# Encoder values projected token-major and carried to three head bands by SBUF-to-SBUF transfers

## Chip, core and metric

The kernel runs on one core of a Trainium2 chip. The metric is the device time of one execution in microseconds (us), lower is better. Before the change the median of three runs is 821.42 us (821.26 to 821.55).

## What is computed

Sixteen images of 37 tokens (one class token and 36 patches), 256 features, go through a patch embedding, a causal attention block with rotary positions, a mixture of 16 experts, a six-layer encoder and a block whose weights are rounded to four bits. The change lies almost wholly in the encoder. Its attention, cut to what matters:

```python
for l in range(LAYERS):                      # 6
    keys = concatenate([past, x], axis=1)    # past is one row of zeros
    q = (x @ Wq.T + bq).reshape(B, T, 16, 16)
    k = (keys @ Wk.T + bk).reshape(B, T + 1, 16, 16)
    v = (keys @ Wv.T + bv).reshape(B, T + 1, 16, 16)
    attn = softmax(where(valid, q k / 4, neg))
    o = (attn v).reshape(B, T, C) @ Wo[l].T + bo[l]
    x = _ln(x + o, ln1_g[l], ln1_b[l])
    ff = gelu(x @ W1[l].T + b1[l]) @ W2[l].T + b2[l]
    x = _ln(x + ff, ln2_g[l], ln2_b[l])
```

## The kernel before

Everything is kept feature-major: 256 features are two chunks of 128 partitions, the tokens lie in the free dimension. The batch is cut into two halves of 8 images (296 tokens, `NHALF`). The encoder is a chain of phases. `phase(x, y)` does the attention of one half (`x`) together with the first normalisation, the hidden layer and the second normalisation of the other half (`y`), so that each half's dependent steps lie beside the other's matrix products. After an entry phase with attention alone (`phase((0, 0), None)`, from 317.21 us), eleven phases have both parts: six with x = half 1, y = half 0 (from 344.25 to 697.54 us) and five with x = half 0, y = half 1 (from 379.67 to 662.44 us). The first kind is called heavy below, since GpSimd also splits W1 and W2 in it, the second light. A last phase has no attention.

Each engine has its own program, in the order in which it is written, and semaphores tie them. fp32 products are made of three fp32r products (high by high, low by high, high by low), so one 128x296 output takes six matmuls. Up to the first feed-forward product a phase with both parts goes:

- TensorE: values `w` (12 matmuls, `project_v`, L807), q of chunk 0 (6), mean of the normalisation (`ln_mean_of`, L725), k0, q1, k1 (18), variance (`ln_var_of`, L735), 16 transposes of the values (`turn_v`, L812), broadcast of the reciprocal (`ln_bcast_of`, L750), two pairs of scores (`scores`, L825), then `up_first` (L1308). The rest is hidden layer, two more pairs of scores, `down`, transposes of the probabilities, values by probabilities (`values`, L861) and the output projection (L877).
- VectorE: the residual sum R and RSUM of y (L2805, L2706), small copies (L2601 to L2609), centring (`ln_centre`, L2094), evacuation of q0 and q1 with three masks each (L2736), reciprocal (L2100), two masked evacuations of the transposed values (`spread_values`, L2111), gain (`scale_gain`, L2712) and low part of the stream (L2582), two more `spread_values`, then maxima, shifts and sums of the softmax.
- ScalarE: `values_out` (L1547) writes each value three times, with a hole for the zero key, into VT; then square (L1531), keys 0, root (L1536), keys 1, high part of the stream (L1842), gelus, exponentials.
- GpSimd: half of the split of W1, the sum of the squares (L2016), the rest of the split, four low parts of the hidden layer (L2054), `normalise` (L1975).
- SyncE: nothing but weight loads in these phases (L694 to L702).

The three copies of a value (`JH` = 3) are rows g*38 to g*38+36 of Ve, each multiplied by a mask that leaves the heads of its band. PSUM banks of the phases are a ring of six, handed out in the order of `phase_order` (L112); `free_bank` (L759) waits for the reader of the job that had the bank before.

Of the kernel before, what the change touches and what calls it, by code (L numbers as in the profile page):

```python
# [16 lines left out]
F32 = mybir.dt.float32  # L17
# [20 lines left out]
KROWS = JH * KEYS  # L38
SCOLS = C * KROWS
# [70 lines left out]
def phase_order(x, y):  # L110
# [12 lines left out]
    att("w", 0, 1)  # L123
# [3 lines left out]
    att("v", 0, 1, 2, 3)  # L127
# [27 lines left out]
def build(nc, a):  # L155
# [8 lines left out]
    with ExitStack() as ctx:  # L164
# [41 lines left out]
        rmask = sb("rmask", [P, JH])  # L206
# [40 lines left out]
        v_, at = cut(at, C * HB * KROWS)  # L247
        VT = v_.rearrange("p (c b g k) -> p c b g k", c=C, b=HB, g=JH)
        ATT_N = at
# [3 lines left out]
        XHL = over("XHL", ARENA_BASE, at, [P, 2, 2, C, NHALF])  # L253
        XH, XL = XHL[:, 0], XHL[:, 1]
        at += 4 * C * NHALF
# [173 lines left out]
        x_ready = sem("x_ready")  # L429
        q_ready, k_ready, v_ready, o_ready = (sem(n) for n in ("q_ready", "k_ready", "v_ready", "o_ready"))  # L430
# [177 lines left out]

        block = ctx.enter_context(nc.Block())
# [3 lines left out]
        def _(sp):  # L613
# [89 lines left out]

            sp.wait_ge(fp4_stored, 32)
# [10 lines left out]
        def _(pe):  # L715
# [91 lines left out]
            def project_v(r, plan, h, pairs, high_count, low_count):  # L807

                two_products(r, plan, [("w", 2 * h + c) for c in range(C)], [pairs(c) for c in range(C)],
                             high_count, low_count)  # L810

            def turn_v(r, plan, h, which=range(4)):  # L812

                for i in which:
                    key = ("v", 4 * h + i)

                    free_bank(r, plan, key, ("w", 2 * h + 1) if i == 0 else None)
                    o = bank_of(plan, key)
                    for b in range(2):
                        for c in range(C):  # L820
                            last = nc.tensor.transpose(o[0:KROWS, b * D + c * P:b * D + (c + 1) * P],
                                                       VT[:, c, 2 * i + b].rearrange("p g k -> p (g k)"), ident)
# [23 lines left out]
            def transpose_probs(r, plan, p, constants=0):  # L846
# [5 lines left out]
                for i in range(2):  # L852
                    for c in range(C):
                        col = (i * C + c) * QROWS
                        last = nc.tensor.transpose(
                            o[0:KROWS, col:col + QROWS],
                            Pr[0:QROWS, (2 * p + i) % PSLOTS, JH * c:JH * (c + 1), :].rearrange("p g k -> p (g k)"),
# [2126 lines left out]
```

## Time and profile before

| | us |
|---|---|
| median of three runs | 821.42 |
| span of the profiled execution | 819.1 |
| PE busy | 801.5 (98%) |
| PE weight load busy | 751.4 (92%) |
| DVE busy | 633.9 (77%) |
| ACT busy | 460.6 (56%) |
| POOL busy | 251.6 (31%) |

The granted clock of TensorE is full over the whole span. A timeline row gives the start, the time from the start of the first to the end of the last instruction, engine, line, output and inputs with their form, and count. Matmuls overlap each other in the pipeline, so what one costs TensorE is the distance of two starts, not its own duration (300 ns for one that follows every 137 ns). A time in brackets is idle time before the row and who ended it. PE is TensorE, DVE VectorE, ACT ScalarE, POOL GpSimd.

### The profile page before, as it was taken

To read this page: it belongs to the slowest core of one execution; us is meant where nothing else is said; L and a number is where in the kernel's file an instruction comes from. 1 tells how busy PE (TensorE), PEld (TensorE's weight loads), DVE (VectorE), ACT (ScalarE), POOL (GpSimd) and SP (SyncE) were. 2 spreads that over 40 slices of the span, in tenths; PEclk is the share of its full clock that TensorE was granted. 3 is DMA by queue.
4 is the path that set the end of the run, shared out by engine and by line. 5 is a ranking of instruction groups with operands and counts; after the bars stand their busy time and mean duration, and the time that the engine had idled before them with its cause. 6 is when DMAs were issued, how large, how long until landed. Compare 5 with 4: busy or idle time off the path is not lost.

```text
span 819.1 us, 16629 instructions
## 1 busy us (share of the span) xinstructions
PE 801.5 (98%) x6060; PEld 751.4 (92%) x6060; DVE 633.9 (77%) x1287; ACT 460.6 (56%) x829; POOL 251.6 (31%) x297
## 2 busy tenths in 40 slices
PE   9999999999999999999999999999999999999988
PEld 8998789999999999899999989999998999999758
DVE  5786693778778876778797887878778787876796
ACT  4386424433333336585786777667687767745421
POOL 0002120410111100364366147335525623633020
PEclk9999999999999999999999999999999999999999
DMA  5010946998889812010210021031012103010001
GB/s 191 1 52 1 373 124 253 328 323 310 317 309 337 321 53 107 1 40 14 100 44 0 17 98 38 13 102 38 4 39 72 38 13 102 26 82 1 1 0 30
DMA packets 18290, 88.36 MB, mean 108 GB/s; under 512 B 3120, under 2 KB 7472, under 8 KB 12240
## 3 DMA queue, kind: packets, MB, share of 16 engines
q1 hardware_dynamic: 18256, 87.90, 30.4%
q8 instruction: 22, 0.36, 0.2%
q14 instruction: 12, 0.10, 0.0%
HBM read 85.05 MB, written 2.84 MB: 107 GB/s over the span
## 4 chain that ended last, share of the span: by engine, by line
PE 47%; issue 23%; POOL 18%; DVE 8%; ACT 3%; DMA 1%; POOLq 0%; SPq 0%; DVEq 0%; ACTq 0%
PE bank L1139 14%; POOL W_L L2000 7%; PE bank L1176 6%; POOL HF_L L2058 4%; POOL arena L1981 3%; POOL WQKV_L L2000 3%; PE bank L746 2%; PE bank L872 2%; PE bank L1185 2%; PE bank L722 2%; PE bank L1049 2%; PE bank L788 1%; POOL SQ L2019 1%; PE bank L1123 1%; PE bank L1490 1%
## 5 line engine op out<-in xcount | busy, mean ns | idle before, releaser
L1139 PE MATMUL bank<-arena 128*128 (+1 forms) x1024 | 117.8, 274 | 0.0
L1139 PEld LDWEIGHTS bank<-arena 128*128 128x128 f32 x1024 | 117.4, 192 | 0.0
L1981 POOL TENSOR_TENSOR arena<-arena,srec 111x456 f32<-111x456 f32 x56 | 52.3, 962 | 125.1 <-DVE srec L2153 125.1
L2000 POOL TENSOR_TENSOR W_L<-LW,W_H 128x256 fp32r<-128x256 f32 x96 | 68.5, 752 | 36.9 <-DVE XHL L2589 33.5
L2058 POOL TENSOR_TENSOR HF_L<-arena,HF_H 128x296 fp32r<-128x296 f32 x48 | 43.8, 937 | 76.7 <-ACT HF_H L1896 76.7
L788 PE MATMUL bank<-XHL,W_H 128*128 128x296 f32 x288 | 65.1, 307 | 0.0
L1896 ACT ACTIVATE arena<-bank,vec 128x296 f32<-128x296 f32 x96 | 48.8, 509 | 20.4 <-PE bank L788 15.4
L2012 POOL TENSOR_TENSOR QW<-QW,arena x14 | 22.4, 1600 | 119.0 <-DVE QW L2490 65.6
L1330 PE MATMUL bank<-HF_L,W_H 128*128 128x296 f32 x192 | 57.4, 299 | 0.0
L1330 PE MATMUL bank<-HF_H,W_H 128*128 128x296 f32 x192 | 57.4, 299 | 0.0
L1330 PE MATMUL bank<-HF_H,W_L 128*128 128x296 f32 x192 | 57.3, 299 | 0.0
L872 PE MATMUL bank<-arena 114*128 114x111 f32 x448 | 55.1, 276 | 0.8 <-issue 0.7
L872 PEld LDWEIGHTS bank<-arena 114*128 114x128 f32 x448 | 53.1, 192 | 2.6 <-issue 1.3
L2165 DVE TENSOR_SCALAR OB<-bank,lvec 96x148 f32<-96x148 f32 x144 | 51.1, 368 | 5.7 <-PE bank L872 3.3
L841 PEld LDWEIGHTS bank<-arena 128*111 128x111 f32 x448 | 52.4, 175 | 1.1
L841 PE MATMUL bank<-arena 128*111 128x114 f32 x448 | 52.7, 260 | 0.0
L2149 DVE TENSOR_REDUCE ssum<-arena 111x12 f32<-111x456 f32 x56 | 32.1, 608 | 23.8 <-ACT arena L1545 23.6
L788 PEld LDWEIGHTS bank<-XHL,W_H 128*128 128x128 f32 x288 | 48.3, 188 | 0.3
L1896 ACT ACTIVATE HF_H<-bank,vec 128x296 fp32r<-128x296 f32 x96 | 48.3, 503 | 0.0
L788 PE MATMUL bank<-XHL,WQKV_H 128*128 128x296 f32 x192 | 45.4, 311 | 0.0
L2138 DVE TENSOR_REDUCE smax<-bank 111x12 f32<-111x456 f32 x56 | 33.9, 622 | 14.4 <-PE bank L841 14.3
L2497 DVE TENSOR_TENSOR EWD_L<-arena,EWD_H 128x2048 fp32r<-128x2048 f32 x16 | 36.9, 2304 | 10.0 <-ACT EWD_H L1758 10.0
(276 smaller groups left out, 2205.4 us busy)
## 6 DMA issues: line engine op xcount, KB each, us to landing
arena<-ew_in SPq DMA_DIRECT2D x16, 2048.0 KB, 9.0
arena<-ew_in SPq DMA_DIRECT2D x16, 1024.0 KB, 7.0
LW<-lw_in SPq DMA_DIRECT2D x12, 1024.0 KB, 5.0
arena<-route SPq DMA_DIRECT2D x32, 185.0 KB, 3.2
LW<-lw_in SPq DMA_DIRECT2D x6, 768.0 KB, 4.3
fp_weights<-arena SPq DMA_DIRECT2D x1, 2048.0 KB, 6.4
arena<-fp_weights SPq DMA_DIRECT2D x1, 2048.0 KB, 7.2
arena<-patches_in SPq DMA_DIRECT2D x2, 864.0 KB, 7.4
```

Source lines behind the costliest of these rows:

```text
L788: last = mm(o, w, x, start=(i == 0), stop=(i == len(pairs) - 1))
L841: last = mm(o[0:QROWS, col:col + KROWS], Qe[:, h, c, bb].rearrange("p s q -> p (s q)"), Ke[:, at_half(plan, h), c, bb].rearrange("p g k -> ...
L872: last = mm(o[:, i * QROWS:(i + 1) * QROWS], Ve[0:KROWS, at_half(plan, h) * HB + b % HB, c * P:(c + 1) * P], PTr[0:KROWS, b % PSLOTS, c, : ...
L1139: last = mm(o[:, m * CAP:(m + 1) * CAP], w[:, kc, mi * P:(mi + 1) * P], xg(kc, e), start=(kc == 0), stop=(kc == C - 1))
L1176: last = mm(bank[4][0:CAP, 0:D], hid_part, w_part, start=(m == 0 and i == 0), stop=(m == EM - 1 and i == 2))
L1330: last = mm(bank_of(plan, keys[c])[:, 0:NHALF], w, moving, start=(m == 0 and i == 0), stop=(m == FM - 1 and i == 2))
L1896: last = f(out[:, m, :], bank_of(plan, ("f1", FM * hy + m))[:, 0:NHALF], ACT.Gelu, bias=vec[:, 3 * C + m:3 * C + m + 1])
L1981: nc.gpsimd.tensor_tensor(v, v, srec[0:QROWS, s:s + 2, :].unsqueeze(3).to_broadcast([QROWS, 2, C * JH, KEYS]), ALU.mult).then_inc(p_ready, 1)
L2000: last = nc.gpsimd.tensor_tensor(low[:, cols], value[:, cols], high[:, cols], ALU.subtract)
L2058: nc.gpsimd.tensor_tensor(HF_L[:, m, :], HF[:, m, :], HF_H[:, m, :], ALU.subtract).then_inc(hl_ready_pool, 1)
L2165: return v.tensor_scalar(dst, src, bias(c)[lo:hi, :], None, ALU.add)
L2497: v.tensor_tensor(EWD_L[s][:, :, :], value, EWD_H[s][:, :, :], ALU.subtract).then_inc(wd_low, 1)
```

## The change

In the encoder the values are projected with the tokens as the stationary operand. Three tiles of three images (the last of two) give 114, 114 and 77 rows (the last three of each are the pad of a 40-row block), each tile 6 matmuls that move 256 weight columns. ScalarE copies them to VTOK. SyncE then issues nine transfers per phase, from SBUF to SBUF: for each of the three bands g and each image i of a tile, 40 rows (37 tokens and 3 that the mask zeroes) to rows g*40 of Ve. The bands are 40 rows apart instead of 38 (`KPAD`), so probabilities and their transposes have 120 rows, with zeroed pads. The images of the first four are masked in place by GpSimd, the last four by VectorE, in one operation each. `turn_v`, `spread_values` and `values_out` remain for the first attention block only. The order in a phase changes too: TensorE makes q0 and k0 together, then q1, mean, k1, two tiles of values, variance, the last tile, scores of pair 0, broadcast, scores of pair 1. VectorE evacuates q0 ahead of the centring. ScalarE puts the square between keys 0 and keys 1 and the root behind keys 1. The jobs `v` leave the encoder's bank ring. SyncE loads the next layer's q, k, v weights when the last value tile is done.

```diff
@@ -36,6 +36,10 @@
 JH = 3
 QROWS = JH * T
 KROWS = JH * KEYS
+KPAD = 40
+VROWS = JH * KPAD
+VTILES = -(-HB // JH)
+XPAD = NHALF + KPAD - T + 1
...
@@ -120,11 +124,10 @@
         if y is not None:
             jobs.extend((kind, y * PER_ROUND[kind] // 2 + i) for i in items)
 
-    att("w", 0, 1)
     for c in range(C):
         att("q", c)
         att("k", c)
-    att("v", 0, 1, 2, 3)
+    att("w", 0, 1)
     att("s", 0, 1)
     for i in range(4):
...
-        v_, at = cut(at, PSLOTS * SCOLS)
-        Pr = v_.rearrange("p (s g k) -> p s g k", s=PSLOTS, k=KEYS)
+        v_, at = cut(at, PSLOTS * C * VROWS)
+        Pr_rows = v_.rearrange("p (s g k) -> p s g k", s=PSLOTS, k=KPAD)
+        Pr = Pr_rows[:, :, :, 0:KEYS]
...
+        VTOK = v_[:, 0:VTILES * D].rearrange("p (t v) -> p t v", t=VTILES)
...
+        V_MOVED = JH * JH * 16
+
+        def first_or_last_values(g4):
+
+            return Ve[0:VROWS, 4 * g4:4 * g4 + 4, :].rearrange("p b (c d) -> p (b c) d", c=C)
+
+        def value_mask():
+
+            return vmask[0:VROWS, :].unsqueeze(1).to_broadcast([VROWS, 4 * C, P])
+
+        def tile_rows(t):
+
+            return (min(JH, HB - t * JH) - 1) * T + KPAD
...
+            def move_values(h, r):
+
+                sp.wait_ge(w_ready, nth("w", 2 * h + 1, r))
+                for g in range(JH):
+                    for i in range(JH):
+                        tiles = -(-(HB - i) // JH)
+                        sp.dma_start(Ve[g * KPAD:(g + 1) * KPAD, i:HB:JH, :], VTOK[i * T:i * T + KPAD, 0:tiles, :]
+                                     ).then_inc(v_landed, 16)
+
+            move_values(0, 1)
             with sp.Fori(1, LAYERS) as l:
-                sp.wait_ge(filled["v"], nth("v", 7, l))
+                move_values(1, l)
+                sp.wait_ge(filled["w"], nth("w", 3, l))
                 load_layer(l)
                 sp.wait_ge(filled["p"], nth("p", 3, l))
                 load_rest(l, "wo", LW_AT["wo"], WO_N, ld_wo)
+                move_values(0, l + 1)
                 sp.wait_ge(filled["f1"], nth_enc("f1", 15, l))
                 load_rest(l, "w1", LW_AT["w1"], W1_N, ld_w1)
                 sp.wait_ge(filled["f2"], nth_enc("f2", 3, l))
                 load_rest(l, "w2", LW_AT["w2"], W2_N, ld_w2)
 
+            move_values(1, LAYERS)
             sp.wait_ge(fp4_stored, 32)
...
+            def values_by_token(r, plan, h, i):
+
+                key = ("w", 2 * h + i)
+                free_bank(r, plan, key)
+                o = bank_of(plan, key)
+                for t in range(2 * i, min(2 * i + 2, VTILES)):
+                    lo, rows, at = t * QROWS, tile_rows(t), t % 2 * D
+                    pairs = [(0, kc, w) for kc in range(C) for w in (WQKV_H, WQKV_L)] + [(1, kc, WQKV_H) for kc in range(C)]
+                    for k, (part, kc, w) in enumerate(pairs):
+                        last = mm(o[0:rows, at:at + D], XHL[:, part, h, kc, lo:lo + rows], w[:, kc, 2 * D:3 * D],
+                                  start=(k == 0), stop=(k == len(pairs) - 1))
+                last.then_inc(filled["w"], 1)
...
-                    if c == 0:
+                    if c == 0 and plan.first:
                         pe.wait_ge(v_ready, nth("v", 4 * h + 3, r))
+                    elif c == 0:
+                        pe.wait_ge((first_masked, last_masked)[g4 % 2], 2 * r + (h - 1))
...
-                    project_v(rx, plan, hx, lambda c: qkv_pairs(2, c), high_count, low_count)
-
-                    def queries_or_keys(c, *kinds):
-                        for kind in kinds:
-                            g = 0 if kind == "q" else 1
-                            key = (kind, 2 * hx + c)
-                            free_bank(rx, plan, key)
-                            products(bank_of(plan, key)[:, 0:NHALF], qkv_pairs(g, c)
-                                     ).then_inc(filled[kind], 1)
-
-                if x:
-                    if y:
-                        pe.wait_ge(proj_added, nth("p", 2 * hy, ry))
-                    queries_or_keys(0, "q")
+                    def query_or_key(kind, c):
+                        key = (kind, 2 * hx + c)
+                        free_bank(rx, plan, key)
+                        products(bank_of(plan, key)[:, 0:NHALF], qkv_pairs("qk".index(kind), c)).then_inc(filled[kind], 1)
+
+                    two_products(rx, plan, [("q", 2 * hx), ("k", 2 * hx)], [qkv_pairs(g, 0) for g in range(2)],
+                                 high_count, low_count)
+                    query_or_key("q", 1)
...
                 if x:
-                    queries_or_keys(0, "k")
-                    queries_or_keys(1, "q", "k")
+                    query_or_key("k", 1)
+                    values_by_token(rx, plan, hx, 0)
...
                     ln_var_of((ly, 0), hy, ones_d)
                 if x:
+                    values_by_token(rx, plan, hx, 1)
                     if entry:
                         ln_bcast_of(LN_ENC, 1)
-                    turn_v(rx, plan, hx)
+                    scores(rx, plan, p0)
...
                 if x:
-                    for i in range(2):
-                        scores(rx, plan, p0 + i)
+                    scores(rx, plan, p0 + 1)
                 if y:
...
-                    values_out(rx, plan, hx)
-                if y:
+                if y and not x:
                     ln_square((ly, 0), hy)
-                if not x:
                     ln_square(LN_FINAL, 0)
...
+                    def values_by_token_out(i):
+
+                        act.wait_ge(filled["w"], nth("w", 2 * hx + i, rx))
+                        o = bank_of(plan, ("w", 2 * hx + i))
+                        tiles = min(2, VTILES - 2 * i)
+                        rows = tile_rows(2 * i)
+                        f(VTOK[0:rows, 2 * i:2 * i + tiles, :].rearrange("p t v -> p (t v)"), o[0:rows, 0:tiles * D], ACT.Copy
+                          ).then_inc(w_ready, 1)
+
                     keys(0)
+                    if y:
+                        ln_square((ly, 0), hy)
+                    keys(1)
                 if y:
                     ln_root((ly, 0), hy)
                 if x:
-                    keys(1)
+                    if y:
+                        act.wait_ge(v_landed, V_MOVED * (lx * 2 + hx))
+                    for i in range(2):
+                        values_by_token_out(i)
                 if y:
                     act.wait_ge(vec_ready, ly + 1)
                     high_stream(hy, xa_count(ly, hy, 0), 0)
...
+            def mask_first_values(h, l):
+
+                pool.wait_ge(v_landed, V_MOVED * (l * 2 + (h + 1)))
+                v = first_or_last_values(0)
+                nc.gpsimd.tensor_tensor(v, v, value_mask(), ALU.mult).then_inc(first_masked, 1)
...
-                    ln_centre((ly, 0), hy)
-                if not x:
-                    ln_centre(LN_FINAL, 0)
+                    if not x:
+                        ln_centre((ly, 0), hy)
+                        ln_centre(LN_FINAL, 0)
                 if x:
                     hx, lx = x
                     rx = lx + 1
                     p0 = HB // 2 * hx
                     for c in range(C):
+                        if y and c == 1:
+                            ln_centre((ly, 0), hy)
...
                     ln_recip((ly, 0), hy)
-                if x:
-                    spread_values(rx, plan, hx, (0, 1))
...
                 if x:
-                    spread_values(rx, plan, hx, (2, 3))
-                if x:
                     row_max(rx, plan, p0)
                     if isinstance(lx, int) and hx + lx == 0:
                         dve.wait_ge(fp4_stored, 32)
+                        link(clear_probability_pads())
...
                     shift(rx, plan, p0 + HB // 2 - 1)
                     if y:
                         low_hidden(2, 3)
+                    dve.wait_ge(v_landed, V_MOVED * (lx * 2 + (hx + 1)))
+                    late = first_or_last_values(1)
+                    v.tensor_tensor(late, late, value_mask(), ALU.mult).then_inc(last_masked, 1)
                     for i in range(0, HB // 2, 2):
```

## Rows read from the trace of the kernel before

**Rows 1.** The page, part 1: busy time, share of the span and instructions.

```profile
PE 801.5 (98%) x6060; PEld 751.4 (92%) x6060; DVE 633.9 (77%) x1287; ACT 460.6 (56%) x829; POOL 251.6 (31%) x297
```

**Rows 2.** Timeline of TensorE in the light phase that starts at 591.76.

```profile
591.76 0.49 PE L803 MATMUL bank<-XHL,WQKV_H 128*128 128x296 f32 x1
...
594.41 0.66 PE L728 MATMUL bank<-RSUM,ones_d 128*128 128x296 f32 x2
...
597.57 0.88 PE L746 MATMUL bank<-ones_d,SQ 128*128 128x64 f32 x6
598.28 1.91 PE L821 MATMUL bank<-const,arena 128*114 128x128 f32 x16
600.03 0.49 PE L755 MATMUL bank<-const,ln_rs 128*128 128x128 f32 x3
...
602.25 0.38 PE L803 MATMUL bank<-XHL,W_H 128*128 128x296 f32 x1
```

**Rows 3.** Timelines of VectorE, ScalarE and GpSimd in the same light phase.

```profile
595.11 0.77 DVE L2097 TENSOR_TENSOR CN<-R,bank 128x592 f32<-128x592 f32 x1 [0.47 <-PE bank L728]
595.80 3.05 DVE L2736 TENSOR_SCALAR arena<-bank,lvec,qmask 128x296 f32<-128x296 f32 x6
...
600.56 0.96 DVE L2716 SCALAR_TENSOR_TENSOR XD<-CN,lvec,bank 128x296 f32<-128x296 f32 x2 [0.35 <-PE bank L755]
...
601.12 0.97 ACT L1849 ACTIVATE XHL<-XD,vec 128x296 fp32r<-128x296 f32 x2 [0.90 <-DVE XD L2716]
...
596.69 0.82 POOL L2019 TENSOR_TENSOR SQ<-SQ 128x296 f32<-128x296 f32 x1 [5.06 <-ACT SQ L1534]
```

**Rows 4.** Timeline of TensorE in the experts: first and last of 24 matmuls over 256 columns.

```profile
301.66 0.28 PE L1176 MATMUL bank<-EWD_L,HH_H 128*74 128x256 f32 x1
...
304.25 0.28 PE L1176 MATMUL bank<-EWD_H,HH_L 128*74 128x256 f32 x1
```

**Rows 5.** Timelines of three engines in the heavy phase that starts at 556.14.

```profile
562.19 0.88 PE L746 MATMUL bank<-ones_d,SQ 128*128 128x64 f32 x6
...
564.66 0.49 PE L755 MATMUL bank<-const,ln_rs 128*128 128x128 f32 x3
...
566.88 0.38 PE L803 MATMUL bank<-XHL,W_H 128*128 128x296 f32 x1
...
559.73 0.77 DVE L2097 TENSOR_TENSOR CN<-R,bank 128x592 f32<-128x592 f32 x1 [0.24 <-PE bank L728]
...
565.86 0.97 ACT L1849 ACTIVATE XHL<-XD,vec 128x296 fp32r<-128x296 f32 x2 [1.01 <-DVE XD L2716]
```

**Rows 6.** Timeline of TensorE: last pair of scores, a heavy and a light phase.

```profile
571.46 0.40 PE L834 MATMUL bank<-amask 128*111 128x456 bf16 x1
...
606.61 0.40 PE L834 MATMUL bank<-amask 128*111 128x456 bf16 x1
```

**Rows 7.** Timelines of VectorE and GpSimd ahead of the softmax sums, light phase.

```profile
608.91 0.83 DVE L2722 TENSOR_TENSOR HF_L<-arena,HF_H 128x296 fp32r<-128x296 f32 x2
...
610.21 1.58 DVE L2722 TENSOR_TENSOR HF_L<-arena,HF_H 128x296 fp32r<-128x296 f32 x2
613.93 1.16 DVE L2149 TENSOR_REDUCE ssum<-arena 111x12 f32<-111x456 f32 x2 [2.14 <-ACT arena L1545]
...
609.64 3.62 POOL L2058 TENSOR_TENSOR HF_L<-arena,HF_H 128x296 fp32r<-128x296 f32 x4 [12.13 <-ACT HF_H L1896]
615.31 3.69 POOL L1981 TENSOR_TENSOR arena<-arena,srec 111x456 f32<-111x456 f32 x4 [2.05 <-DVE srec L2153]
```

**Rows 8.** Timelines of TensorE and GpSimd in the entry phase.

```profile
317.21 0.39 PE L803 MATMUL bank<-XHL,WQKV_H 128*128 128x296 f32 x1
...
331.69 4.14 POOL L1981 TENSOR_TENSOR arena<-arena,srec 111x456 f32<-111x456 f32 x4 [37.17 <-DVE srec L2153]
```

**Rows 9.** The page, part 6: DMA issues, KB of each, us from issue to landing.

```profile
LW<-lw_in SPq DMA_DIRECT2D x6, 768.0 KB, 4.3
...
arena<-patches_in SPq DMA_DIRECT2D x2, 864.0 KB, 7.4
```

More of the change, by code:

```diff
@@ L251, in build @@
         HF = v_.rearrange("p (m t) -> p m t", m=FM)
-        XHL = over("XHL", ARENA_BASE, at, [P, 2, 2, C, NHALF])
-        XH, XL = XHL[:, 0], XHL[:, 1]
-        at += 4 * C * NHALF
+        XHL = over("XHL", ARENA_BASE, at, [P, 2, 2, C, XPAD])
+        XH, XL = (XHL[:, k, :, :, 0:NHALF] for k in range(2))
+        at += 4 * C * XPAD
         W1_H = over("W1_H", ARENA_BASE, at, [P, C, HID])
@@ L805, in two_products, with turn_v @@
                             last.then_inc(filled[key[0]], 1)
[L807 to L812, printed above, removed]
+            def values_by_token(r, plan, h, i):
[9 more added lines that the diff above has]
+                last.then_inc(filled["w"], 1)
+            def turn_v(h, which):
                 for i in which:
                     key = ("v", 4 * h + i)
-                    free_bank(r, plan, key, ("w", 2 * h + 1) if i == 0 else None)
-                    o = bank_of(plan, key)
+                    free_bank(0, BLOCK0, key, ("w", 2 * h + 1) if i == 0 else None)
+                    o = bank_of(BLOCK0, key)
                     for b in range(2):
                         for c in range(C):
-                            last = nc.tensor.transpose(o[0:KROWS, b * D + c * P:b * D + (c + 1) * P],
+                            last = nc.tensor.transpose(o[0:VROWS, b * D + c * P:b * D + (c + 1) * P],
                                                        VT[:, c, 2 * i + b].rearrange("p g k -> p (g k)"), ident)
@@ L2239, in masks @@
                 link(v.tensor_scalar(qmask[:, 1, :], qmask[:, 0, :], HD ** -0.5, None, ALU.mult))
-                three_bands(rmask, KEYS)
+                p1 = cst("iota_col")
+                for g in range(JH):
+                    link(v.tensor_scalar(vrow[:, g:g + 1], p1, float(g * KPAD), None, ALU.is_gt))
+                    last = v.scalar_tensor_tensor(vrow[:, g:g + 1], p1, float(g * KPAD + T), vrow[:, g:g + 1],
+                                                  ALU.is_le, ALU.mult)
+                link(last)
                 for j in range(JH):
                     dst = vmask[:, :].rearrange("p (i d) -> p i d", d=HD)[:, j::JH, :]
-                    last = v.tensor_copy(dst, rmask[:, j:j + 1].unsqueeze(2).to_broadcast([P, dst.shape[1], HD]))
+                    last = v.tensor_copy(dst, vrow[:, j:j + 1].unsqueeze(2).to_broadcast([P, dst.shape[1], HD]))
                 link(last)
@@ L2349, in _ @@
             ln_recip(LN_ATT0, 1)
[L2350 removed]
+            spread_values(0, (0,))
             block0_scale(1)
             rope(0, 1, (1,))
[L2353 removed]
+            spread_values(0, (1,))
             block0_low(1)
[L2355 removed]
+            spread_values(0, (2, 3))
             rope(1, 0, (0,))
@@ L2373, in _ @@
             row_recip(0, 2)
-            spread_values(0, BLOCK0, 1, (0,))
+            spread_values(1, (0,))
             row_sum(0, 3)
             row_recip(0, 3)
-            spread_values(0, BLOCK0, 1, (1, 2))
+            spread_values(1, (1, 2))
             row_max(0, BLOCK0, 4)
@@ L2394, in _ @@
             row_recip(0, 7)
-            spread_values(0, BLOCK0, 1, (3,))
+            spread_values(1, (3,))
             dve.wait_ge(proj_added, 2)
```

62 lines of the change are left out of this document (33 added, 29 removed).

## Prediction

> **What bounds the kernel now.** I read the page's busy line first. TensorE is busy 98% of the span [rows 1], so the first guess is that each matmul column taken away is time won. Then I read the timelines of one phase, engine by engine, for what TensorE waits on at the end of each step. In a light phase it runs from 591.76 to the first feed-forward product at 602.25, 10.49 us, nearly without a gap [rows 2]. Three chains of the normalisation cross this stretch: mean (594.41), variance (597.57), broadcast (600.03). Between mean and variance VectorE centres at 595.11, ScalarE squares, GpSimd adds from 596.69 to 597.51, and the variance starts at 597.57 [rows 2, 3]: 2.46 us from centring to variance, and TensorE starts it 0.06 us after GpSimd is done. So this chain, not the 18 matmuls beside it, sets the start already. Between broadcast and feed-forward VectorE scales at 600.56 and ScalarE makes the high part from 601.12, two operations in 0.97 [rows 3]. Its first half lands at about 601.63, so the feed-forward product could start at about 601.73, 1.70 us after the broadcast started. It starts at 602.25, so two pairs of scores hide this chain with 0.5 us to spare. The question for the change is what hides these chains in the new order.
>
> **Part 1, matmuls.** Removed in each of 12 phases: 12 matmuls over 296 columns for the values, at the distance of 0.137 us that such matmuls keep in this trace; I work it out from the 18 matmuls plus mean between 594.41 and 597.57, less the mean's 0.5 and the wait of 0.2 (2.46/18) [rows 2]. That is 1.64 us. Removed too: 16 transposes, 600.03 - 598.28 = 1.75 us [rows 2]. Added: 18 matmuls over 256 columns. 23 distances of such take 304.25 - 301.66 + 0.118 = 2.71, 0.118 each [rows 4], so 2.12 us. Net -1.27 us, and -1.23 with one more switch from fp32 to fp32r. If nothing else bound, 12 x 1.23 = 14.8 us would be won.
>
> **Part 2, the variance in a light phase.** VectorE is idle for 0.47 before it centres at 595.11, so it is free at 594.64 [rows 3]. The new order puts q0 ahead of the centring: three of the six operations that take 3.05 together, 1.5 us [rows 3]. q0 is filled by then (10 matmuls after 591.76, about 593.3), so it runs 594.64 to 596.15. The centring moves by 1.04, and the variance, 2.46 behind it, to 598.61. TensorE would be ready much sooner: from the mean it has 6 matmuls (0.82) and two value tiles (12 x 0.118 = 1.42) in the place of 18 (2.46), so 0.22 earlier than today's 597.37, at 597.15. It waits 1.5 us. The 1.75 us of transposes were behind the variance and don't help here.
>
> **Part 3, from the variance to the feed-forward.** Behind 598.61 come variance 0.71 (598.28 - 597.57), third value tile 0.78 (6 x 0.118 and the switch), one pair of scores 0.98 (half of 602.25 - 600.03 - 0.33, rounded up with its bf16 mask product), then the broadcast at 601.08. The root and reciprocal fit in (ScalarE has keys 1 from about 597.6 to 599.1, before the variance is done at 599.3). Only one pair of scores is left behind the broadcast, 0.33 + 0.98 = 1.31 us, against the 1.70 us that the chain needs. The feed-forward starts at 601.08 + 1.70 = 602.78, 0.53 later than today [rows 2, 3]. From there the order and the matmuls are as before, and TensorE is full. So a light phase gets longer by 0.5 us: saving 1.23 becomes a loss. Five phases: +2.6.
>
> **Part 4, heavy phases.** Here VectorE is idle only 0.24 before 559.73 [rows 5], so 1.5 us of q0 push the centring by 1.27, the variance from 562.19 to 563.46, the broadcast to 563.46 + 2.47 = 565.93. The high part starts 1.20 after the broadcast (565.86 - 564.66) and its half takes 0.5, so 1.81 to the product: 567.74 against 566.88, +0.86 [rows 5]. One gain: the fourth pair of scores starts 4.58 behind the first feed-forward product in the heavy phase, 4.36 in the light one [rows 5, 6, 2]. The 0.22 is a wait for a shift that VectorE does behind the last `spread_values`. Those are gone and the wait with them. 0.64 x 6 = +3.8.
>
> **Part 5, what is hidden.** ScalarE loses two operations over 888 elements and gains 512 + 256, and it waits for nothing there. VectorE loses four evacuations of 512, and gains one mask over 1024 elements from SBUF to SBUF. Its price: 0.83 for two of 296, 1.58 for the same two while GpSimd works [rows 7], so 1.3 to 2.7 us; I take 1.3, since it is mostly one long operation. It stands behind the low parts that end at 611.79, ahead of the sums that wait until 613.93: 2.14 us of cover [rows 7]. GpSimd's mask is priced by `normalise`, 3.69/4 = 0.92 per 456 elements, 2.1 us for 1024 (by the fp32r subtractions of 3.62/4 per 296, 3.1). It has 12 us of idle ahead of 609.64 in a light phase, and behind it 2.05 before `normalise` [rows 7]. I cost both at nothing; without cover they cost what they take, up to 2 us a phase. The small pads and masks before the encoder: +0.1.
>
> The wait that is new is for the nine transfers. 960 KB of 1 KB runs have no row of their kind. Nearest below: 768 KB in 4.3 us, so 5.4. Nearest above, runs of 1152 B: 864 KB in 7.4, so 8.2 [rows 9]. I take 7, nearer to the short runs, from the first issue. In a light phase the last value tile is copied by about 600.7, so they land at 607.7, before GpSimd's 609.64 and VectorE's 611.79. Queued behind them on SyncE is only the load of the next q, k, v weights, which nobody needs before the phase ends.
>
> The row of 768 KB and that of 864 KB spread over 128 partitions. The Trainium skill (DMA: Bandwidth & Descriptors, "Why a DMA increments its semaphore by 16 and not by 1") says that a transfer uses the largest number of DMA engines up to 16 that divides its outer dimension, so 40 rows get ten. An estimate by that page, 5.4 x 1.6 = 8.6 us, would still be covered in eleven phases. No row of the trace before has 40 rows.
>
> **Part 6, the entry phase.** It has no feed-forward to hide anything. Today `normalise` starts at 331.69 [rows 8]. New: q, k and three tiles are done about 317.21 + 24 x 0.137 + 2.12 = 322.6, copied by 323.3, landed by 330.3. VectorE masks 330.3 to 331.6, then sums (1.16) and reciprocals to about 333.1; GpSimd masks to 332.4, and if the two shut each other out, to 333.7. So `normalise` starts at 333.1 to 335.2 and all that follows is later by that much: +1.4 to +3.5, and with 5.4 or 8.2 us of transfer -0.2 to +4.7. I take +2.4.
>
> The two rows of 0.83 and 1.58 show that VectorE and GpSimd slow each other on SBUF [rows 7]. The Trainium skill (SBUF — State Buffer, "SBUF: two separate sides") calls it an exclusive lock for the whole instruction when a VectorE operation has two SBUF inputs; by that the masks here run one after the other, the upper half of the range just given.
>
> **Sum.** 2.6 + 3.8 + 0.1 + 2.4 = +8.9 us. The profiled span is 819.1, 2.3 below the median of 821.42, and none of that is touched. 821.4 + 8.9 = 830.3.
>
> **Rivals.** (a) *The busy share decides*, faster: the waits of parts 2 and 3 don't arise and 14.8 is won, less 2.4 at the entry: 809. It needs the variance's input 1.5 us earlier than the rows say, at 597.15 in the light phase; even with q0 for nothing it comes at 597.57. Chance 0.07. (b) *q0 doesn't push the centring*, faster: if VectorE has q0 done before the mean is there, the variance stays at 597.57, the feed-forward starts at 597.57 + 2.47 + 1.70 = 601.74, -0.5 a light phase, -0.4 - 0.2 a heavy one, -6.1 + 2.5: 818. It decides at a q0 start of 593.6, when VectorE still adds residuals. Chance 0.13. (c) *Half of the push*, 821 to 825, the chain after the broadcast shorter than read: 0.15. (d) *Values come late in every phase*: if the transfers take over 11 us or the masks 2 us more than covered, each of 11 phases waits 1 to 2 us at the sums: +11 to +22 on the forecast, 841 to 852. For it: short runs, nine issues, one queue; against it: 9 us between copy and first need. Chance 0.15. The forecast, 825 to 836, has 0.5.
>
> **Numbers.** The range runs from 817 to 839: it holds the forecast, (b), (c) and the near end of (d). 0.2% is 1.6 us, about what a measurement of this kernel can tell from no change. Faster: (a), (b): 0.2. Same: part of (c): 0.1. Slower: 0.7.
>
> **What would show it.** In the timeline after: an idle of about 1.5 us before the variance matmuls, q0's evacuation ahead of the centring that waits for nothing, feed-forward starts about 11.0 and 11.6 us into the phase (now 10.5 and 10.7); phases of 35.6 and 36.2 us. Wrong if the centring starts within 0.1 us of the mean's end, or if TensorE waits at the probabilities' transposes for over 0.5 us a phase (d).

## Result and profile after

The changed kernel takes 849.0 us (848.6 to 849.3) against 821.3 us before, a ratio of 1.0336 with a 95% interval of 1.0322 to 1.0351. It is slower, as forecast, but by 27.7 us where 8.9 were worked out, and outside the range. The profiled span is 847.3 us, 28.2 more than before [rows 1]. The page's busy line of the changed kernel:

```profile
PE 800.4 (94%) x5940; PEld 742.3 (88%) x5940; DVE 634.1 (75%) x1255; ACT 452.4 (53%) x829; POOL 295.5 (35%) x309
```

TensorE has 120 matmuls fewer and is busy about as long, in a span that is 28 us longer: the time is in its gaps. GpSimd has 44 us more. The trace's sum of waits names the gaps (columns: engine, line, who ended the wait; us in total, times, longest us); L779 is the variance, L896 the transposes of the probabilities, L836 the feed-forward:

```profile
PE bank L896 <- POOL arena L2031: 13.2, 24, 5.4
PE bank L779 <- POOL SQ L2069: 13.1, 11, 1.4
PE bank L836 <- ACT XHL L1886: 3.1, 11, 0.4
```

The variance has 11 waits that it did not have. The front of the light phase that starts at 611.14, in TensorE's timeline (answers to [rows 2]):

```profile
617.83 0.88 PE L779 MATMUL bank<-ones_d,SQ 128*128 128x64 f32 x6 [1.18 <-POOL SQ L2069]
618.52 0.32 PE L849 MATMUL bank<-WQKV_H,XHL 128*77 128x256 f32 x1
...
619.26 0.35 PE L875 MATMUL bank<-amask 128*111 128x456 bf16 x1
...
620.23 0.49 PE L788 MATMUL bank<-const,ln_rs 128*128 128x128 f32 x3
...
621.91 0.40 PE L836 MATMUL bank<-XHL,W_H 128*128 128x296 f32 x1 [0.22 <-ACT XHL L1886]
```

TensorE waits 1.18 us for the squares, and the feed-forward starts 10.77 us into the phase (10.49 before). The last value tile takes 0.74 us, 0.78 was reckoned. In the heavy phase from 573.80 the same two rows are:

```profile
580.97 0.88 PE L779 MATMUL bank<-ones_d,SQ 128*128 128x64 f32 x6 [1.39 <-POOL SQ L2069]
...
585.16 0.40 PE L836 MATMUL bank<-XHL,W_H 128*128 128x296 f32 x1 [0.33 <-ACT XHL L1886]
```

7.17 and 11.36 us into the phase, against 6.05 and 10.74 before. The larger part of the loss comes later in a phase. VectorE, GpSimd and SyncE of the light phase (answers to [rows 3] and [rows 7]); L2156 is the centring, L2806 the evacuation of q, L2790 and L2117 are low parts, L2833 and L2075 the masks, L2208 the sums, L2031 `normalise`, L720 the transfers:

```profile
613.91 1.57 DVE L2806 TENSOR_SCALAR arena<-bank,lvec,qmask 128x296 f32<-128x296 f32 x3
615.40 0.76 DVE L2156 TENSOR_TENSOR CN<-R,bank 128x592 f32<-128x592 f32 x1
...
628.69 0.83 DVE L2790 TENSOR_TENSOR HF_L<-arena,HF_H 128x296 fp32r<-128x296 f32 x2
...
629.98 3.13 DVE L2790 TENSOR_TENSOR HF_L<-arena,HF_H 128x296 fp32r<-128x296 f32 x2
633.04 1.84 DVE L2833 TENSOR_TENSOR arena<-arena,vmask 120x1024 f32<-120x1024 f32 x1
634.80 1.15 DVE L2208 TENSOR_REDUCE ssum<-arena 111x12 f32<-111x456 f32 x2
...
629.13 2.66 POOL L2075 TENSOR_TENSOR arena<-arena,vmask 120x1024 f32<-120x1024 f32 x1 [11.36 <-DMA arena<-arena]
631.75 4.59 POOL L2117 TENSOR_TENSOR HF_L<-arena,HF_H 128x296 fp32r<-128x296 f32 x4
636.29 3.92 POOL L2031 TENSOR_TENSOR arena<-arena,srec 111x456 f32<-111x456 f32 x4
...
619.86 7.30 SPq L720 DMA_DIRECT2D arena<-arena  x9
```

The nine issues run for 7.30 us, the last bytes are there at 629.13, 9.27 us after the first issue. GpSimd masks for 2.66 and so begins its low parts 20.6 us into the phase (17.9 before). The mask lies across VectorE's second pair of low parts, which takes 3.13 us (1.58 before). The sums, ahead of which VectorE stood idle for 2.14 us before [rows 7], follow without a gap, 23.7 us into the phase (22.2 before), and `normalise` starts 25.2 us into it (23.6 before). What TensorE feels of this is seen in the products of `down` (L1373), which need the low parts:

```profile
635.19 0.30 PE L1373 MATMUL bank<-HF_L,W_H 128*128 128x296 f32 x1
635.62 0.41 PE L1373 MATMUL bank<-HF_H,W_H 128*128 128x296 f32 x1
...
636.39 0.41 PE L1373 MATMUL bank<-HF_H,W_H 128*128 128x296 f32 x1
...
638.13 0.92 PE L896 MATMUL bank<-const,arena 111*120 111x111 f32 x8
```

GpSimd's third and fourth low part end at 635.56 and 636.33, each 0.06 us ahead of a product that starts late. The 48 products take 7.43 us (6.55 before), and two waits of 0.17 and 0.57 us for `normalise` follow (one of 0.34 before).

Last the entry phase (answers to [rows 8]), SyncE, VectorE, GpSimd and TensorE:

```profile
323.55 7.53 SPq L720 DMA_DIRECT2D arena<-arena  x9
...
332.98 1.23 DVE L2833 TENSOR_TENSOR arena<-arena,vmask 120x1024 f32<-120x1024 f32 x1 [3.62 <-DMA arena<-arena]
...
333.02 3.39 POOL L2075 TENSOR_TENSOR arena<-arena,vmask 120x1024 f32<-120x1024 f32 x1 [37.96 <-DMA arena<-arena]
336.38 4.39 POOL L2031 TENSOR_TENSOR arena<-arena,srec 111x456 f32<-111x456 f32 x4
...
337.38 0.99 PE L896 MATMUL bank<-const,arena 111*120 111x111 f32 x4 [5.35 <-POOL arena L2031]
```

And the table of stretches of the same part (stretch, its length, then busy time and instructions of PE, PEld, DVE, ACT, POOL; the third number from the end is the granted clock):

```profile
325.00:332.00 7.00, 7.00 (x64) 6.80 (x63) 4.05 (x9) 2.29 (x4) 0.00 (x0) 1.00 0.43 135
332.00:337.30 5.30, 0.03 (x1) 0.00 (x0) 4.29 (x11) 0.00 (x0) 4.28 (x3) 0.97 0.03 7
337.30:343.00 5.70, 5.35 (x26) 5.03 (x27) 3.76 (x5) 2.44 (x6) 3.47 (x4) 0.50 0.00 0
343.00:350.90 7.90, 7.10 (x52) 6.54 (x52) 4.23 (x13) 5.72 (x6) 2.78 (x4) 0.95 0.01 2
```

TensorE stands still for 5.35 us and then works at the lower level, 1.2 GHz, over the whole stretch of 5.7 us.

Where the 28.2 us of span are, by the starts of the phases: the entry phase 33.5 us long (27.0 before), +6.5; a light phase 36.93 (35.08), +1.85; a heavy one 37.34 (35.62), +1.72; not every phase follows the pattern (the first light one takes 37.92 and two heavy ones 37.6, the first heavy one is only 0.7 longer than before, the last 3.0); the eleven take +21.5 together, and the head +0.2.

### The profile page after: what moved, and what is told of

It is laid out like the page before. It is cut to its first block, busy times and chain, and to the rows that moved or that the text cites. A ratio compares the mean times of both kernels' runs of the same rounds, so it can differ in the third digit from the quotient of the medians.

```text
span 847.3 us, 16522 instructions
## 1 busy us (share of the span) xinstructions
PE 800.4 (94%) x5940; PEld 742.3 (88%) x5940; DVE 634.1 (75%) x1255; ACT 452.4 (53%) x829; POOL 295.5 (35%) x309
## 4 chain that ended last, share of the span: by engine, by line
PE 45%; issue 23%; POOL 19%; DVE 7%; ACT 2%; SPq 2%; DMA 1%; POOLq 0%; DVEq 0%; ACTq 0%
PE bank L1182 13%; POOL W_L L2050 6%; PE bank L1219 5%; POOL arena L2031 4%; POOL HF_L L2117 4%; PE bank L755 3%; POOL WQKV_L L2050 2%; PE bank L779 2%; PE bank L915 2%; PE bank L1228 2%; PE bank L1092 2%; SPq L720 2%; POOL SQ L2069 1%; PE bank L1166 1%; PE bank L1527 1%
## 5 line engine op out<-in xcount | busy, mean ns | idle before, releaser
L2031 POOL TENSOR_TENSOR arena<-arena,srec 111x456 f32<-111x456 f32 x56 | 54.7, 1003 | 65.8 <-DVE srec L2212 65.8
L2075 POOL TENSOR_TENSOR arena<-arena,vmask 120x1024 f32<-120x1024 f32 x12 | 35.3, 2939 | 108.4 <-DMA arena<-arena 108.4
L1373 PE MATMUL bank<-HF_H,W_H 128*128 128x296 f32 x192 | 60.8, 317 | 4.3 <-POOL HF_L L2117 1.8
L1373 PE MATMUL bank<-HF_L,W_H 128*128 128x296 f32 x192 | 57.5, 299 | 0.0
L1373 PE MATMUL bank<-HF_H,W_L 128*128 128x296 f32 x192 | 57.4, 299 | 0.0
L915 PE MATMUL bank<-arena 120*128 120x111 f32 x448 | 55.6, 278 | 0.8 <-issue 0.7
L915 PEld LDWEIGHTS bank<-arena 120*128 120x128 f32 x448 | 53.8, 194 | 2.5 <-issue 1.2
L1599 ACT ACTIVATE arena<-bank 120x444 f32<-120x444 f32 x56 | 28.7, 538 | 46.8 <-PE bank L896 45.2
L2117 POOL TENSOR_TENSOR HF_L<-arena,HF_H 128x296 fp32r<-128x296 f32 x48 | 51.7, 1108 | 0.0
L2069 POOL TENSOR_TENSOR SQ<-SQ 128x296 f32<-128x296 f32 x24 | 19.5, 811 | 90.4 <-ACT SQ L1571 90.4
L779 PE MATMUL bank<-ones_d,SQ 128*128 128x64 f32 x264 | 35.9, 278 | 14.0 <-POOL SQ L2069 13.1
```

The source lines that it names most:

```text
L779: last = mm(ln_bank(seq, h)[:, at:at + VAR_W], sq[:, h, c, t0:t0 + P], ones[:, 0:VAR_W], start=(c == 0), stop=(c == nch - 1))
L915: last = mm(o[:, i * QROWS:(i + 1) * QROWS], Ve[0:VROWS, at_half(plan, h) * HB + b % HB, c * P:(c + 1) * P], PTr[0:VROWS, b % PSLOTS, c, : ...
L1373: last = mm(bank_of(plan, keys[c])[:, 0:NHALF], w, moving, start=(m == 0 and i == 0), stop=(m == FM - 1 and i == 2))
L2031: nc.gpsimd.tensor_tensor(v, v, srec[0:QROWS, s:s + 2, :].unsqueeze(3).to_broadcast([QROWS, 2, C * JH, KEYS]), ALU.mult).then_inc(p_ready, 1)
L2117: nc.gpsimd.tensor_tensor(HF_L[:, m, :], HF[:, m, :], HF_H[:, m, :], ALU.subtract).then_inc(hl_ready_pool, 1)
```

## Experiments

Theory from the trace: the front order (q0 ahead of the centring) costs about 0.5 us a phase and GpSimd's and VectorE's masks, which come when the transfers are done, the other 1.3; the entry phase pays for both in full. Rivals: the transfers' lateness alone, the masks' length alone, or the front order for all of it. e2, e3, e4 and e11 leave out part of the work, and e9 the values of the last five tokens; what is left out stands with each. The lengths of a light phase, a heavy phase and the entry phase are read from TensorE's timeline in the same way for each kernel:

| kernel | us | ratio to before | light | heavy | entry |
|---|---|---|---|---|---|
| before | 821.3 | 1 | 35.08 | 35.62 | 27.04 |
| after | 849.0 | 1.0336 | 36.93 | 37.34 | 33.51 |
| e10, before with q0 first | 833.5 | 1.0147 (1.0130 to 1.0164) | 36.19 | 36.72 | 27.07 |
| e1, after with the centring first | 841.3 | 1.0239 (1.0222 to 1.0256) | 36.35 | 36.48 | 33.72 |
| e2, three transfers | 832.9 | 1.0136 (1.0119 to 1.0153) | 35.54 | 37.06 | 28.59 |
| e3, both masks small | 829.4 | 1.0096 (1.0080 to 1.0113) | 35.54 | 36.12 | 30.68 |
| e11, GpSimd's mask small | 830.8 | 1.0118 (1.0101 to 1.0135) | 35.53 | 36.11 | 31.59 |
| e9, nine transfers of 32 rows | 842.0 (one time) | | 36.32 | 37.02 | 31.42 |
| e4, e2 and e3 together | 824.9 | 1.0038 (1.0024 to 1.0053) | 35.54 | 36.13 | 25.90 |
| e6, no masks | 826.3 | 1.0063 (1.0046 to 1.0080) | 35.69 | 36.26 | 25.84 |
| e7, e6 and centring first | 817.8 | 0.9957 (0.9941 to 0.9974) | 35.08 | 35.15 | 25.80 |
| e8, e7 and broadcast first | 811.4 | 0.9878 (0.9862 to 0.9895) | 34.51 | 34.60 | 25.81 |

**e10, the one edit of part 2 in the kernel before.**

```diff
-                    ln_centre((ly, 0), hy)
...
                     for c in range(C):
+                        if y and c == 1:
+                            ln_centre((ly, 0), hy)
                         dve.wait_ge(filled["q"], nth_enc("q", 2 * hx + c, rx))
```

> The kernel before with one edit: VectorE evacuates q of chunk 0 ahead of the centring instead of behind it. Nothing else of the change. By part 2 of the prediction the push is 1.04 us in a light phase and 1.27 in a heavy one, nothing behind the variance takes it up, so 5 x 1.04 + 6 x 1.27 = 12.8: 834 us. With the pushes that the changed kernel's variance showed against the same kernel with the centring first (0.6 and 1.1): 5 x 0.6 + 6 x 1.1 = 9.6: 831 us. If q0 is done before the mean is there, no change: 821 us. Half of the push: 828 us.

833.5 us, +12.2. TensorE in the light phase from 600.33:

```profile
607.20 0.88 PE L746 MATMUL bank<-ones_d,SQ 128*128 128x64 f32 x6 [1.11 <-POOL SQ L2019]
...
611.89 0.38 PE L803 MATMUL bank<-XHL,W_H 128*128 128x296 f32 x1
```

The variance starts 6.87 us into the phase (5.81 before) and the feed-forward 11.56 (10.49): a push of 1.07 in the light phase and, likewise, 1.12 in the heavy one, and the phases are longer by just that (1.1). Part 2's 1.04 is right; part 4's 1.27 was 0.15 too much. Rivals (b) and (c) are out: the push comes whole.

**e1, the same edit undone in the changed kernel.**

```diff
-                        if y and c == 1:
+                        if y and c == 0:
                             ln_centre((ly, 0), hy)
```

> One edit on the changed kernel: VectorE centres ahead of evacuating q0, as before the change. Theory (front order): the variance in a light phase goes back from 6.69 us into the phase to about 5.85, in a heavy phase from 7.17 to 6.05, the first feed-forward product to 9.97 and 10.3, and since the transfers and masks follow TensorE, all of it is won: 11 phases by 0.8 to 1.0, so 849.0 - 10 = 839. Rival (masks alone): the front isn't what costs, what is won there is lost again at the masks, 847 to 849.

841.3 us, -7.7, where 839 was expected. The variance is at 6.10 (light) and 6.04 (heavy). The light phase keeps 1.27 us over before, though its feed-forward starts at 10.18, ahead of the 10.49 of before: the front was not the main loss.

**e2, three transfers instead of nine.**

```diff
-                for g in range(JH):
+                for g in range(1):
```

> Only the three transfers of band 0 are issued instead of nine; the values of the other two bands are left out (their rows of Ve are zeroed once), the masks and all waits stay. Theory (late landing): the last transfer lands about 4.5 us after the values are copied instead of 9.4, the masks run in the idle time ahead of the hidden layer's low parts, and each of 11 phases wins the 1.3 us that it lost between the first feed-forward product and the second mean; the entry phase wins 5 us for the landing and 1 for the clock: 849 - 14 - 5 = 830. Rival (the masks cost by their length, wherever they stand): the 11 phases stay as they are, only the entry phase wins, 843.

832.9 us, -16.2. In the light phase from 600.10 (SyncE and GpSimd) the last bytes are there 4.4 us after the first issue:

```profile
608.83 2.44 SPq L721 DMA_DIRECT2D arena<-arena  x3
...
613.20 2.41 POOL L2080 TENSOR_TENSOR arena<-arena,vmask 120x1024 f32<-120x1024 f32 x1 [6.46 <-DMA arena<-arena]
```

This phase takes 35.54 us, with both masks whole: early enough, they cost nothing. The heavy one is not healed: there GpSimd, VectorE and TensorE show

```profile
579.68 2.41 POOL L2080 TENSOR_TENSOR arena<-arena,vmask 120x1024 f32<-120x1024 f32 x1
...
581.15 2.27 DVE L2795 TENSOR_TENSOR HF_L<-arena,HF_H 128x296 fp32r<-128x296 f32 x2
...
584.10 0.40 PE L1375 MATMUL bank<-HF_H,W_H 128*128 128x296 f32 x1 [0.82 <-DVE arena L2206]
```

The data wait for GpSimd here, which is splitting W2; the mask comes right behind that, now across VectorE's first pair of low parts (2.27 us for what takes 0.84), and TensorE waits ahead of `down` instead of in it and behind it.

**e3, both masks small, nine transfers.**

```diff
-            return Ve[0:VROWS, 4 * g4:4 * g4 + 4, :].rearrange("p b (c d) -> p (b c) d", c=C)
+            return Ve[0:VROWS, 4 * g4:4 * g4 + 4, :].rearrange("p b (c d) -> p (b c) d", c=C)[:, 0:1, 0:32]
```

> Both masks shortened to 32 of 1024 elements (most of the masking is left out); nine transfers and all waits stay. Theory (late landing times length): with nothing to do behind the wait, the lateness costs nothing in the 11 phases, as the landing at 18.0 us is ahead of the low parts: -14; in the entry phase the wait stays and 2.5 of the masks' 3.4 us go: 832. Rival (the wait itself blocks, the landing is what costs): little is won, 845.

829.4 us, -19.6. Both kinds of phase are at the forecast's lengths (35.54 and 36.12 against 35.6 and 36.2), with the transfers as late as in the changed kernel. So the lateness costs nothing by itself in eleven phases; it does in the entry phase, 30.7 us.

**e11, only GpSimd's mask small.** The same edit in `mask_first_values` alone.

> The changed kernel with GpSimd's mask over 32 elements instead of 1024 (the first four images' values keep the heads of the other bands); VectorE's mask is whole. Both masks small gave 829.4, 19.6 us less than the changed kernel. Theory, GpSimd's long mask is what costs most, since it delays its own low parts and normalise and, while it runs, the low parts of VectorE take 3.1 us instead of 1.6: 831 to 834 us, VectorE's low parts back to 1.6 to 2.2 us. Rival, the two masks cost alike: 838 to 840 us. Rival, VectorE's mask ahead of the sums is the costly one: 844 to 848 us.

830.8 us, -18.2 of the 19.6: with GpSimd's mask small nearly all is won. The reverse, only VectorE's mask small, was not run, so what that alone would win is open. VectorE's timeline in the light phase from 599.15:

```profile
616.71 0.84 DVE L2790 TENSOR_TENSOR HF_L<-arena,HF_H 128x296 fp32r<-128x296 f32 x2
...
618.00 0.83 DVE L2790 TENSOR_TENSOR HF_L<-arena,HF_H 128x296 fp32r<-128x296 f32 x2
618.75 1.22 DVE L2833 TENSOR_TENSOR arena<-arena,vmask 120x1024 f32<-120x1024 f32 x1
...
621.75 1.16 DVE L2208 TENSOR_REDUCE ssum<-arena 111x12 f32<-111x456 f32 x2 [1.79 <-ACT arena L1582]
```

The low parts take 0.83 instead of 3.13, VectorE's own mask 1.22 instead of 1.84, and 1.79 us of idle are left ahead of the sums. Here part 5 is right about VectorE's mask, price (1.3) and cover both (beside GpSimd's low parts, as in the changed kernel, the same mask takes 1.84); the 1.4 us that it still costs against e3 lie mostly in the entry phase (31.59 against 30.68).

**e9, nine transfers of 32 rows.**

```diff
-                        sp.dma_start(Ve[g * KPAD:(g + 1) * KPAD, i:HB:JH, :], VTOK[i * T:i * T + KPAD, 0:tiles, :]
+                        sp.dma_start(Ve[g * KPAD:g * KPAD + 32, i:HB:JH, :], VTOK[i * T:i * T + 32, 0:tiles, :]
```

> The changed kernel with nine transfers of 32 rows each instead of 40 (the values of the last five tokens of every image are left out; the target is cleared once). The bytes fall by a fifth, and 32 is a multiple of 16. Theory one, the nine issues on SyncE set the landing, about 0.8 us each: the masks still start about 9.3 us after the first issue (8.9 to 9.6) and the time stays at 847 to 850 us. Rival, the transfers themselves are slow because 40 rows reach only ten of the sixteen DMA engines: the landing comes at least 2 us earlier (7.4 us or less after the first issue), and the time falls to 838 to 843 us. A landing earlier by 0.5 to 1 us with issues as long as before would mean that only the tail behind the last issue depends on the rows.

A first form of it, e5, without the clearing of the target, gave no result.

The landing comes 7.26 us after the first issue (9.27), so the number is that of the rival, and so is the time. But the issues changed too, which neither theory had. All 108 issues of the changed kernel and of e9 (ns min/median/max, first and last start):

```profile
L720 SPq DMA_DIRECT2D arena<-arena x108: 767/768/1876, 323.5 to 739.6; - x108
```

```profile
L721 SPq DMA_DIRECT2D arena<-arena x108: 585/598/1747, 324.3 to 731.6; - x108
```

Eight issues that are 0.17 us shorter are 1.4 of the 2.0 us. The time from the last issue's start to the landing fell from 2.7 to 2.1 us. That the issues set the pace, and not the transfers behind them, is shown by e2: with three transfers the landing comes as long after the last issue's start as with nine (2.7 us both), so nothing piles up behind the issues. Theory one was right in that and wrong in holding an issue's length fixed. The time of 842.0 us tells more. With a landing at 16.0 us of the light phase, just where part 5 had put it (15.9), the phase is still 36.32 and not 35.54. GpSimd, VectorE and TensorE in the phase from 606.73:

```profile
622.72 2.39 POOL L2080 TENSOR_TENSOR arena<-arena,vmask 120x1024 f32<-120x1024 f32 x1 [9.35 <-DMA arena<-arena]
...
624.29 2.15 DVE L2795 TENSOR_TENSOR HF_L<-arena,HF_H 128x296 fp32r<-128x296 f32 x2
...
627.12 0.40 PE L1375 MATMUL bank<-HF_H,W_H 128*128 128x296 f32 x1 [0.66 <-DVE arena L2206]
```

The mask now shuts out the first pair of low parts, as in e2's heavy phase.

**e4, few transfers and small masks.** The edits of e2 and e3.

> Three transfers and short masks together (two bands of values and most of the masking left out). Theory: what is left is the front order, 11 phases by 0.1 to 0.5 us, so 821.3 + 4, about 825, entry phase shorter than before the change by about 1 us. Rival: if the tokens-stationary products or the 120-row probabilities cost something themselves, 830 or more.

824.9 us: this is parts 1 to 4 with part 5 at nothing. The phases show +5.4 for the front (0.46 x 5 + 0.51 x 6) and -1.1 for the entry phase, 4.3; the time shows +3.5, so 0.8 is won elsewhere. It lies in the first heavy phase, which takes 34.8 us where before has 35.4 and the push would give 35.9; why is not shown.

**e6, no masks, nothing left out.** ScalarE writes each head band's columns into a zeroed tile of its own, so that the transfers carry masked values; GpSimd clears the zero key's probability behind each part of `normalise`.

```diff
+                        for g in range(JH):
+                            dst = VTOK[g][0:rows, 2 * i:2 * i + tiles, :].rearrange("p t (c n) -> p (t c) n", c=C)
...
+                            last = f(cut_(dst), cut_(src), ACT.Copy)
...
-                        sp.dma_start(Ve[g * KPAD:(g + 1) * KPAD, i:HB:JH, :], VTOK[i * T:i * T + KPAD, 0:tiles, :]
+                        sp.dma_start(Ve[g * KPAD:(g + 1) * KPAD, i:HB:JH, :], VTOK[g][i * T:i * T + KPAD, 0:tiles, :]
```

> Full result without masks: ScalarE writes the columns of each band of heads into one of three token-major tiles (zeroed once), so the transfers carry masked values; the zero key's probability, 1 of 38, is cleared by GpSimd; the values' matmuls wait for the transfers themselves. Order of the changed kernel. Theory: the nine issues and the late landing (about 18 us into a phase) cost nothing when nobody but the values' matmuls (30 us in) waits for them; 11 phases as in the run with short masks (35.5 and 36.1), entry phase 25.9, and 0.1 us per pair for the clearing: 825 to 828. Rival: token-major values cost beyond the masks (the transfers' own traffic, the 18 matmuls), over 832.

826.3 us with all nine transfers. The masks' share of the loss is gone; a phase is 0.13 to 0.15 us longer than e4's.

**e7 and e8.** e7 adds e1's edit to e6. e8 also puts the broadcast ahead of the first pair of scores, so that two pairs lie beside its chain again:

```diff
                 if x:
+                    if y:
+                        scores(rx, plan, p0)
                     scores(rx, plan, p0 + 1)
```

> The same, and VectorE centres ahead of q0. The front of the phase wins 0.6 (light) and 1.1 us (heavy) as it did with the masks: -10 against the run without masks, about 816, faster than before the change.

> The same, and the broadcast ahead of the first pair of scores, so that two pairs lie behind it again as before the change. The first feed-forward product then follows TensorE's own work and not the chain of 1.7 us: another 0.4 us in each of 11 phases, about 811. Rival: ScalarE, with six short copies in place of two between root and high part, holds the chain, and nothing is won over the run before this.

817.8 and 811.4 us. e8 was measured a second time:

> The best version so far once more, on another chip and in more rounds: the head bands' columns written by ScalarE into three zeroed tiles, no masks, the centring ahead of q0, the broadcast ahead of the first pair of scores. Expected as before, 811.4 us (810.6 to 812.2), a ratio of 0.988 to the kernel before with an interval that excludes 0.991.

811.7 us (811.6 to 811.9), a ratio of 0.9883 (0.9867 to 0.9900). Its page and its waits:

```profile
PE 787.5 (97%) x5940; PEld 738.0 (91%) x5940; DVE 610.7 (75%) x1243; ACT 453.6 (56%) x877; POOL 255.8 (32%) x356
```

```profile
PE bank L890 <- POOL arena L2035: 4.5, 12, 0.4
PE bank L773 <- POOL SQ L2071: 4.4, 11, 0.6
```

The waits at the probabilities are those that before has too (4.0 in 12), those at the variance are down from 13.1 to 4.4. This version beats both kernels: 9.6 us less than before.

## Why the prediction was right and wrong

- **Part 1, right.** A value tile takes 0.74 us (0.78). As forecast, none of the 1.23 us a phase was won while the chains bound: TensorE waits 13.1 us at the variance alone. e8, with shorter chains, has 4.4 us of them left and gains 1.0 us in a heavy phase (34.60) and 0.57 in a light one (34.51).
- **Part 2, right.** Centring 4.26 us into the light phase (3.35 before), +0.91 for +1.04; TensorE waits 1.18 and 1.39 for 1.5. e10 shows the mechanism alone, +12.2 us in a kernel that has nothing behind it to take it up.
- **Part 3, right in the mechanism.** Broadcast to feed-forward takes 1.68 us in the light phase (1.70), and e8 turns it: with two pairs of scores behind the broadcast each phase is 0.55 us shorter than e7's. The phase grew by 0.46 without the masks (e4) for 0.53, but in part by luck: the feed-forward starts only 0.28 us later, and 0.17 more is lost between it and the third pair of scores (1.89 us, 1.72 before), where the prediction had "the order and the matmuls are as before, and TensorE is full".
- **Part 4, right in the mechanism.** +0.51 (e4) for +0.64: the feed-forward starts 0.62 us later for 0.86, and from it to the fourth pair of scores 0.09 us is gained for 0.22.
- **Part 5, wrong, and the largest error: 14 us by the two patterns (11 x 1.3), 16 by the eleven phases (21.5 less the front's 5.4).** Three terms. The transfers took 9.3 us and not 7: nine issues of 0.8 us each occupy SyncE for 7.3, and they went into the estimate by bytes alone. By itself this costs nothing in the eleven phases (e3); with the landing back at the forecast's place (e9) 0.6 us of the light phase's 1.4 and 0.3 of the heavy one's 1.2 are won. The step that failed is the cover: "It has 12 us of idle ahead of 609.64" and "I cost both at nothing". The idle was there, yet the mask can't use what lies ahead of its data: behind my own landing time, 607.7, only 1.9 us were left for an operation of 2.1 (2.66 in fact). Behind the true one nothing was left: GpSimd's own low parts start 2.7 us later and run 1.0 us longer, more than the 2.05 us behind them cover, and the last two hold up `down`. And I gave the rows 0.83 and 1.58 [rows 7] to VectorE's mask as its price, and not to VectorE's low parts as what GpSimd's mask would do to them: they grew to 3.13. e9 has the landing that was forecast and still loses 0.8 us a phase. Which of the two, GpSimd's late low parts or VectorE's stretched ones, would have cost how much alone in the changed kernel is not told apart; e9 and e2's heavy phase show the second by itself. This is near rival (d), "each of 11 phases waits 1 to 2 us", at the price of 1.2 to 1.4, and the sign named for it came: TensorE waits 0.7 us a phase at the probabilities' transposes (13.2 less the entry's 5.4, over 11). But its condition, transfers over 11 us or masks 2 us over the cover, was not what brought it, and more than half of the wait is in `down`. It should have carried more than 0.15. The range to 839 doesn't hold "the near end of (d)" either, since (d) begins at 841.
- **Part 6, wrong in size.** +6.5 for +2.4. `normalise` starts at 336.38: the landing adds 2.4 us to the estimate and the masks exclude each other, 1.23 beside 3.39. From its start to the end of the phase it was 12.56 us before [rows 8] and is 14.54 now: 2.0 us more, for the clock that fell to 1.2 GHz over the gap. In e4 and e6, where no gap there is over 0.8 us and the clock stays full, the same stretch takes 12.56 and 12.59 us. The prediction had no such term.

With the masks' 1.3 for eleven phases and the entry's 6.5, the same sum gives 5.4 + 14.3 + 6.5 = 26.2 of the 28.2 us; 0.2 is in the head, and the rest in the phases that don't follow the pattern, which no run explains.

## What to carry to other kernels

Idle time covers a moved operation only from the moment its input is there, so count cover from the landing and not from the engine's last work; and ask of each new operation on GpSimd which of its own operations stand behind it and which of VectorE's it will lie across, because the price is paid there. A row of transfers is to be priced by the queue's issues first: nine at 0.8 us were 7.3 us, whether one carried 120 or 80 KB. Where a mask only sorts columns, let the engine that copies out of PSUM anyway write them sorted (e6): both masks went, and 0.13 to 0.15 us a phase came in their place (e6 against e4).

## What the hardware showed

- An issue of 40 rows between two places in SBUF holds SyncE's queue for 768 ns (all but three of 108 are under 0.9 us), one of 32 rows 598 ns; a plain weight load of 128 rows is issued in 0.33 us. It isn't the runs or the bytes that count here: six of the nine issues carry three runs of 1 KB a row and three carry two, and both kinds have a median of 768 ns.
- The time from the first of nine issues to the landing is 9.3 us, with three issues 4.4: 0.8 per issue. From the last issue's start it is 2.7 us in both. The Trainium skill (DMA: Bandwidth & Descriptors, "Why a DMA increments its semaphore by 16 and not by 1") would put 40 rows on ten DMA engines and 32 rows on sixteen. The traces agree: the landing semaphore is raised in 11 steps a transfer in the changed kernel (99 for nine), one and then ten, and in 16 a transfer in e9 (144 for nine). What ten engines in place of sixteen cost is not shown apart from what eight rows more cost, neither in the 0.17 us an issue nor in the 0.6 us between 2.7 and 2.1 behind the last issue.
- VectorE's pair of low parts takes 0.83 us alone and 2.15 to 3.13 across GpSimd's mask of 2.4 to 2.7 us; at an equal share of a port it would be at most 1.7. The Trainium skill (SBUF — State Buffer, "SBUF: two separate sides") calls it an exclusive lock for the whole instruction; by that rule a pair waits for the rest of the mask, and the trace agrees: the first low part starts at 629.98 and ends at 632.11, 0.3 us behind the mask's end at 631.79, and in the entry phase GpSimd's mask, which starts 0.04 us behind VectorE's, takes 3.39 (2.39 in e9).
- After 5.35 us without a matmul TensorE's granted clock was 0.50 over the next 5.7 us. From 350.9 us on, where no wait of TensorE is over 1.4 us before the last phase's end, the mean granted clock of each stretch is 1.00.
